# A post-norm decoder layer: x1 and x2 turned by transposing DMA loads instead of by TensorE

## The reference

```python
x1 = layernorm(x  + causal_self_attention(x))        # 16 heads of 32
x2 = layernorm(x1 + cross_attention(x1, ctx))        # one head of 512
# recurrence over the 16 items as time steps, 224 rows as batch:
f = sigmoid(x2[t] @ wf.T + c @ uf.T + bf)
i = sigmoid(x2[t] @ wi.T + c @ ui.T + bi)
g = tanh   (x2[t] @ wc.T + c @ uc.T + bc)
c = f * c + i * g
# output gate, with the last c, for all items:
h = tanh(x2 @ wo.T + c @ uo.T + bo)
out = layernorm(x2 + h)
```

## Time and profile before

| | |
|---|---|
| median of 3 runs | 1476.96 us |
| profiled execution | 1476.7 us, span 1474.8 us, mean granted TensorE clock 0.985 |
| TensorE matmul / weight load | 98% / 85% of the span |
| VectorE / ScalarE / GpSimd | 65% / 43% / 37% |
| DMA | 131.11 MB, 27.8% of 16 engines' span |

### The profile page before, as it was taken

The page is one execution under the profiler, slowest core; times in us unless marked ns, Lnnn a source line. Parts: engine busy times, 40 slices in busy tenths (PEclk is TensorE's granted clock), DMA queues, the critical chain, the costliest instruction groups (busy, mean ns, idle before and its releaser), DMA issues.

```text
span 1474.8 us, 28858 instructions
## 1 busy us (share of the span) xinstructions
PE 1439.7 (98%) x10322; PEld 1254.5 (85%) x10322; DVE 961.9 (65%) x1999; ACT 641.1 (43%) x1890; POOL 541.1 (37%) x429
## 2 busy tenths in 40 slices
PE   6999999999979999999999999999999999999997
PEld 3677777777779999999999999999999999999886
DVE  4578888888767786787778762353455434555697
ACT  4477777777444444444444433322222322222232
POOL 2444555555464656465646552000000000001264
PEclk9899999999999999999999998899999999999999
DMA  6113322324247443334333313200000001000253
GB/s 193 42 52 90 98 76 87 87 80 161 66 155 196 150 156 129 129 129 159 124 130 129 128 32 111 83 26 1 25 25 0 25 0 31 22 7 29 81 192 122
DMA packets 71611, 131.11 MB, mean 89 GB/s; under 512 B 7218, under 2 KB 15410, under 8 KB 71540
## 3 DMA queue, kind: packets, MB, share of 16 engines
q1 hardware_dynamic: 71540, 130.17, 27.8%
HBM read 106.30 MB, written 22.02 MB: 87 GB/s over the span
## 4 chain that ended last, share of the span: by engine, by line
PE 90%; issue 4%; POOL 3%; DVE 2%; SPq 0%; DMA 0%; ACT 0%; POOLq 0%; DVEq 0%
PE banks L1434 15%; PE banks L1453 10%; PE banks L933 9%; PE banks L917 9%; PE banks L307 7%; PE banks L946 6%; PE banks L904 5%; PE banks L1455 5%; PE banks L275 5%; PE banks L256 2%; PE banks L287 2%; PE banks L262 2%; PE banks L235 2%; PE banks L890 2%; POOL o_r L1977 1%
## 5 line engine op out<-in xcount | busy, mean ns | idle before, releaser
L433 ACT ACTIVATE s_p<-banks,a_nmax 112x224 f32<-112x224 f32 (+1 forms) x512 | 198.8, 417 | 94.4 <-DVE a_nmax L519 94.4
L697 POOL TENSOR_TENSOR s_p<-s_p,a_rinv 112x896 f32<-112x896 f32 (+1 forms) x128 | 165.0, 1311 | 166.9 <-DVE a_rinv L527 161.3
L1395 POOL CAST m_hi<-w_raw 128x2048 fp32r<-128x2048 f32 x1 | 2.3, 2257 | 422.6 <-PE banks L1434 422.6
L1638 DVE TENSOR_TENSOR f_gate<-banks,f_xg_early 128x448 f32<-128x448 f32 x45 | 28.1, 624 | 194.4 <-PE banks L1455 194.4
L1257 POOL TENSOR_TENSOR x_cx_lo<-s_cx_raw,x_cx_hi 125x512 fp32r<-125x512 f32 x96 | 120.5, 1292 | 36.1 <-ACT x_cx_hi L1045 36.1
L1543 ACT ACTIVATE f_gate<-f_gate 128x448 f32<-128x448 f32 x90 | 52.1, 579 | 182.5 <-DVE f_gate L1641 182.5
L534 DVE COPY a_pt<-banks 112x448 f32<-112x448 f32 x128 | 79.2, 619 | 61.7 <-PE banks L275 61.6
L433 ACT ACTIVATION_READ_ACCUMULATOR s_p<-banks,a_nmax 112x1 f32 x512 | 113.8, 222 | 0.0
L275 PEld LDWEIGHTS banks<-identity,s_p 112*112 112x112 f32 x768 | 86.6, 134 | 30.5 <-issue 9.3
L275 PE MATMUL banks<-identity,s_p 112*112 112x112 f32 x768 | 106.2, 262 | 0.9 <-DVE a_pt L534 0.9
L518 DVE TENSOR_REDUCE a_nmax<-banks 112x1 f32<-112x224 f32 x256 | 96.8, 378 | 12.6 <-PE banks L262 12.3
(11 more groups left out here) (239 smaller groups left out, 3694.2 us busy)
## 6 DMA issues: line engine op xcount, KB each, us to landing
s_ct_raw<-in_ct SPq DMA_DIRECT2D x16, 1500.0 KB, 6.9
s_cx_raw<-in_cx SPq DMA_DIRECT2D x16, 1500.0 KB
a_xt<-in_xt SPq DMA_DIRECT2D x16, 448.0 KB, 3.9
a_xrow<-in_x SPq DMA_DIRECT2D x16, 448.0 KB, 3.6
a_xres<-in_x SPq DMA_DIRECT2D x16, 448.0 KB, 4.6
x_scratch<-a_xn SPq DMA_DIRECT2D x16, 448.0 KB, 3.1
x_scratch<-x_xn SPq DMA_DIRECT2D x16, 448.0 KB, 3.8
out<-o_y SPq DMA_DIRECT2D x28, 256.0 KB, 2.0
```

The source lines that it names most:

```text
L433: e = act.activation((p1 if c else p0)[:, g, h, :], src, ACT.Exp, bias=nmax[:, g % 2, c, h:h + 1], accum_out=rsum[:, g % 2, c, h:h + 1])
L697: pool.tensor_tensor(p[:, g, :, :], p[:, g, :, :], inv, ALU.mult).then_inc(norm_done, 1)
```

## The change

Beside the fp32 rows, x1 and x2 are now also stored in DRAM as 16-bit halves: `x1_halves` and `x2_halves` have 2T rows for an item, row 2t holding the lower 16 bits of each value of row t and row 2t+1 the upper. A transposing load of such an item, 448 rows by 512 columns of 2-byte elements, leaves on each feature's partition the two halves of each value beside one another, which read as fp32 are the turned item. All `x1_turn` but the first, and `next_turn`, `x_turn` and `turn`, are gone; roundings and low halves read the loaded tile in SBUF, in one instruction of 896 columns instead of two of 448 out of PSUM.

For that: ScalarE separates halves (`separate` for x2, from the normalised item in SBUF, and `separate_ahead` for x1, from an extra load of x1 two items ahead), 2048 columns each, and SyncE stores them. Extra waits keep buffers apart; the load of the wc weight moves from step 2 to the end of cross-attention, since its buffer holds the new tiles. In the softmax the biased maximum and the shift move from VectorE to ScalarE.

In the output gate the turned tiles are loaded 4 slots deep; low halves move from VectorE to GpSimd, the residual from GpSimd to VectorE, and the norm from VectorE to ScalarE, as `y = r * rstd + (-mean * rstd)` with a small instruction for the offset ahead of it; the power of tile n runs one tile earlier in the order. Products use 8 banks instead of 6. The constant -0.5 is made once.

```diff
             def load_rows(b, odd):
                 wait(sp, x1b_done, b - 1)
-                wait(sp, x1t_done, b - 1)
+                if isinstance(b, int) and b in (2, 3):
+                    sp.wait_ge(x1t_done, b - 1)
                 wait(sp, rowbias_done, b - 1)
                 sp.dma_start(x1_raw[odd][:], x1[b].rearrange("(c p) d -> p c d", p=R)).then_inc(x1_in[odd], 16)
 
             def loads(b, odd):
                 wait(sp, ctl_done, KC * b)
                 sp.dma_start(ct_raw[:], io["ct"][b].rearrange("(k p) t -> p k t", p=128)).then_inc(ct_in, 16)
-                if within(b + 1, B):
+                if not (isinstance(b, int) and b == 1):
+                    wait(sp, ahead_stored, 16 * (b - 1))
+                    wait(sp, x1tl_done, b)
+                    if within(b + 1, B):
+                        load_rows(b + 1, 1 - odd)
+                    sp.dma_start_transpose(x1t[:].bitcast(U16), x1_halves[b]).then_inc(x1t_in, 16)
+                elif within(b + 1, B):
                     load_rows(b + 1, 1 - odd)
                 if within(b - 3, B):
                     store(b - 3)
                 wait(sp, cxl_done, XC * b)
                 sp.dma_start(cx_raw[:], io["cx"][b].rearrange("(c p) d -> p c d", p=XR)).then_inc(cx_in, 16)
+                if within(b + 1, B):
+                    wait(sp, ahead_done, b)
+                    sp.dma_start(x1_halves[b + 1].rearrange("(c p w) d -> p c w d", p=R, w=2), ahead_halves[:]).then_inc(ahead_stored, 16)
+                if within(b + 2, B):
+                    rows_ahead(b + 2)
+
+            def rows_ahead(b):
+                sp.dma_start(ahead[:], x1[b].rearrange("(c p) d -> p c d", p=R)).then_inc(ahead_in, 16)
 
             def store(b):
                 sp.wait_ge(xn_done, TC * (b + 1))
                 sp.dma_start(x2[b].rearrange("(c p) d -> p c d", p=R), xn[:]).then_inc(stored, 16)
+                sp.wait_ge(halves_done, b + 1)
+                sp.dma_start(x2_halves[b].rearrange("(c p w) d -> p c w d", p=R, w=2), halves[:]).then_inc(halves_stored, 16)
...
             sp.wait_ge(shared.stored, 16 * B)
+            rows_ahead(2)
...
+            sp.wait_ge(x1tl_done, B)
+            sp.wait_ge(ahead_stored, 16 * (B - 2))
+            load_weight(sp, raw[2], raw_in[2], io["wc_t"])
             for b in range(2):
                 sp.wait_ge(x1b_done, B - 1 + b)
-                sp.wait_ge(x1t_done, B - 1 + b)
                 sp.wait_ge(rowbias_done, B - 1 + b)
-                sp.wait_ge(stored, 16 * (b + 1))
-                sp.dma_start(x1_raw[b][:], x2[b].rearrange("(c p) d -> p c d", p=R)).then_inc(opening.x2_in[b], 16)
...
                     s(b)
-                if within(b + 1, B):
-                    x1_turn(b + 1, 1 - odd, i + 1 + odd)
-                if isinstance(b, int) and b == B:
-                    next_turn(0)
-                    next_turn(1)
+                if isinstance(b, int) and b == 0:
+                    x1_turn(1, 1, 1)
                 if isinstance(b, int) and b == B - 1:
...
+                if not (isinstance(b, int) and b == 1):
+                    wait(act, x1t_in, 16 * (b - 1))
+                    wait(act, zt_done, b)
+                    act.activation(x1t_hi[:], x1t[:], ACT.Copy).then_inc(x1th_done, 1)
+                    return
...
             def exp(b):
                 wait(act, pt_done, XC // 2 * b)
                 wait(act, rinv_done, b)
+                wait(act, rowbias_done, b + 1)
                 for c in range(TC):
+                    wait(act, max_done, TC * b + c + 1)
+                    act.activation(biased_max[:, c:c + 1], smax[:, c:c + 1], ACT.Identity, bias=rowbias[:, c:c + 1]).then_inc(biased_done, 1)
+                    wait(act, biased_done, TC * b + c + 1)
+                    wait(act, exp_done, TC * (b - 1) + c + 1)
+                    act.activation(shift[:, c:c + 1], biased_max[:, c:c + 1], ACT.Identity, scale=-1.0, bias=rowbias[:, c:c + 1])\
+                       .then_inc(shift_done, 1)
                     wait(act, shift_done, TC * b + c + 1)
                     act.activation(p[:, c, :].rearrange("p (a t) -> p a t", a=2), ps_s[0:R, 2 * c:2 * c + 2, 0:XH],
                                    ACT.Exp, bias=shift[:, c:c + 1], accum_out=rsum[:, c:c + 1]).then_inc(exp_done, 1)
 
+            def separate_ahead(b):
+
+                wait(act, ahead_in, 16 * (b - 1))
+                wait(act, ahead_stored, 16 * (b - 2))
+                act.activation(ahead_halves[:], ahead[:].bitcast(U16).rearrange("p c (d w) -> p c w d", w=2), ACT.Copy).then_inc(ahead_done, 1)
+
+            def separate(b):
+
+                wait(act, xn_done, TC * (b + 1))
+                wait(act, halves_stored, 16 * b)
+                act.activation(halves[:], xn[:].bitcast(U16).rearrange("p c (d w) -> p c w d", w=2), ACT.Copy).then_inc(halves_done, 1)
...
                     cxh(b)
+                if within(b - 2, B) and not (isinstance(b, int) and b == B):
+                    separate(b - 2)
+                if within(b, B):
                     exp(b)
                 if within(b + 1, B):
                     x1th(b + 1)
+                if within(b + 2, B):
+                    separate_ahead(b + 2)
...
             def next_columns_low(b):
-                bank = ps_s[:, 2 * b:2 * b + 2, :]
                 dve.wait_ge(opening.xth_done, b + 1)
-                for k in (0, 2):
-                    v = dve.tensor_tensor(opening.xt_lo[:, k:k + 2, b, :], bank[:, k // 2, 0:2 * T].rearrange("p (k t) -> p k t", k=2),
-                                          opening.xt_hi[:, k:k + 2, b, :], ALU.subtract)
-                v.then_inc(opening.xtl_done, 1)
+                dve.tensor_tensor(opening.xt_lo[:, :, b, :], opening.x2t[b][:], opening.xt_hi[:, :, b, :], ALU.subtract)\
...
-                sp.dma_start(x2_raw[:, a, :, :], x2[b].rearrange("(c p) d -> p c d", p=R)).then_inc(x2_in[a], 16)
+                    wait(sp, xtl_done, b - 1)
...
-                act.activation(xt_hi[:, 0:2, a, :], turned(b, 0), ACT.Copy)
-                act.activation(xt_hi[:, 2:4, a, :], turned(b, 2), ACT.Copy).then_inc(xth_done, 1)
+                act.activation(xt_hi[:, :, a, :], x2t[:, a, :, :], ACT.Copy).then_inc(xth_done, 1)
...
+                dve.tensor_tensor(xt_lo[:, :, a, :], x2t[:, a, :, :], xt_hi[:, :, a, :], ALU.subtract).then_inc(xtl_done, 1)
...
-    SLOTS, BANKS = 8, 6
+    SLOTS, BANKS, XT = 8, 8, 4
...
+            def load_turned(n):
+                if n >= TILES:
+                    return
+                if n >= XT:
+                    sp.wait_ge(xtl_done, n - XT + 1)
+                sp.dma_start_transpose(xt[:, n % XT, :, :].bitcast(U16), x2_half_rows[2 * P * n:2 * P * n + 2 * P, :]).then_inc(xt_in[n % XT], 16)
+
+            sp.wait_ge(closing.xtl_done, B)
+            for n in range(XT):
+                load_turned(n)
+            sp.wait_ge(closing.w_split[3], 1)
             for n in range(4):
                 load(n)
-            sp.wait_ge(closing.w_split[3], 1)
+            sp.wait_ge(closing.w_split[4], KC)
             for n in range(4, SLOTS):
                 load(n)
+            for n in range(XT, XT + 3):
+                load_turned(n)
             sp.wait_ge(base_done, 1)
             for j in range(TURNS):
                 for p, q, t, n in pieces(j):
                     sp.dma_start(turned[p:p + n, j, :], base[t:t + n, q, :]).then_inc(turned_in[j // 2], 16)
-            for n in range(SLOTS, TILES):
-                load(n)
+            load_turned(XT + 3)
+            for n in range(SLOTS, TILES + SLOTS):
+                load_turned(n)
+                if n < TILES:
+                    load(n)
                 store(n - SLOTS)
-            for n in range(TILES - SLOTS, TILES):
-                store(n)
             for s in range(4):
                 sp.wait_ge(stored[s], 16 * (TILES // 4))
...
         def xth(act, n):
             if n >= TILES:
                 return
-            act.wait_ge(xt_done, n + 1)
+            act.wait_ge(xt_in[n % XT], 16 * (n // XT + 1))
             if n >= 2:
                 act.wait_ge(o_done, n - 1)
-            act.activation(xt_hi[:, n % 2, :, :], turn_bank(n), ACT.Copy).then_inc(xth_done, 1)
-
-        def xtl(dve, n):
+            act.activation(xt_hi[:, n % 2, :, :], xt[:, n % XT, :, :], ACT.Copy).then_inc(xth_done, 1)
+
+        def xtl(pool, n):
             if n >= TILES:
                 return
-            dve.wait_ge(xth_done, n + 1)
-            dve.tensor_tensor(xt_lo[:, n % 2, :, :], turn_bank(n), xt_hi[:, n % 2, :, :], ALU.subtract).then_inc(xtl_done, 1)
...
+            def norm(n):
+                if n < 0:
+                    return
+                s = n % 4
+                act.wait_ge(rstd_done, n + 1)
+                act.wait_ge(veps_done, 2 * n + 2)
+                act.activation(offset[:, s, :], negative[:, s, :], ACT.Identity, scale=rstd[:, s, :]).then_inc(offset_done, 1)
```

(95 more changed lines are left out.)

213 lines of the change are left out of this document (92 added, 121 removed).

## The result

The changed kernel takes 1470.8 us (median of 5 runs, 1468.2 to 1474.6) against 1476.96: a ratio of 0.9961, 95% interval 0.9943 to 0.9979, so 0.4% faster: 6.2 us by these medians, 5.8 by the ratio. Its profiled execution took 1470.8 us, its span is 1469.1.

The account below looks back on a forecast made before the run. TensorE's own instruction stream was taken to bound cross-attention and recurrence. 1476.7 less 25.5 before the output gate, plus 16.2 in it and 0.3 from profiled execution to median, gave 1467.7, so 1468 us; range 1447 to 1500.

Parts of the forecast that it names:

- Part 1: Cross-attention: TensorE loses the turns of x1 for items 2 to 15, 14 x 0.77 = 10.8 us gained.
- rival C: Cross-attention: the gain is eaten by ScalarE's extra 4.9 us an item, time 1475 to 1479; chance 0.10.
- the turned item is issued behind a 1500 KB load that lands in 6.9 us: Cross-attention: leaves at least 4 us for the 448 KB turning load, 115 GB/s before ScalarE waits.
- Part 2: First cross-attention softmax: TensorE's wait falls from 8.10 to 1.9 us, transposes gain 1.5; together 7.7 gained.
- Part 3: Cross-attention into recurrence: turns of x2 go, but colliding low halves and the late uf load cost more; net 3.4 us lost.
- Part 4: Recurrence: 9.2 us gained from turns of items 4 to 15, about 1.2 from three gate tiles at its end.
- Part 5: Output gate: VectorE's residual and GpSimd's low half collide, a tile every 3.7 us; gate 101.5 us, cost +16.2.
- and directly behind it the next low half 1.24: Output gate: GpSimd's low half directly follows its power, so VectorE's residual waits it out; loop 3.55 us, 3.7 with hand-overs.
- rival A: Output gate: the collision hardly binds; gate 85 us, time 1451 (1445 to 1457); chance 0.17.
- the loop of 7.4 us for two tiles: Output gate, last 12 tiles, lead 1: even without the collision, product through low half and hand-overs take 7.4 us per two tiles.
- B: Output gate: turning loads are slow and transfers bind; time 1503 at 80 GB/s, 1557 at 50; chance 0.22.
- D: Output gate: TensorE, idle a quarter of each tile, gets the lower clock; gate 154 us, time 1520; chance 0.03.

Follow-up runs that it names:

- The split load: Changed kernel with every load of cx_raw issued as two, rows 0 to 111 and 112 to 124 of each chunk, same bytes: 1456.8 us, ratio 0.9872.
- the test alone: Kernel before with only the softmax's biased maximum and shift moved to ScalarE, ahead of the exponential: 1469.57 us, ratio 0.9960.
- The test with uf early: Changed kernel with the load of uf issued ahead of the last two items' stores: 1464.75 us, ratio 0.9921.
- a lead of 2: Changed kernel with LEAD 2 instead of 1 for the output gate's last twelve tiles: 1457.8 us, ratio 0.9882.

## Why the prediction came out near, and which steps failed

1468 against 1470.8 is luck: two terms were wrong by more than 11 us each, with opposite signs. The faster result itself was forecast (9.3 us, about 6 measured), but it is no larger than what the softmax part gains alone.

**Part 1** (10.8 for 14 turns): the term per item is right, 0.82 measured, and ScalarE's extra work was covered, so rival C is out. The step that failed is "the turned item is issued behind a 1500 KB load that lands in 6.9 us". I looked at the load of ct_raw alone. In the same queue stand cx_raw, the store of the halves that the transposing load itself waits for, and at item 3 the weights. In the kernel before, cx_raw delayed nothing that was needed soon; the changed kernel puts a store and a dependent load behind it. The loss at items 2 and 3 was 13 us. The split load shows the cause, since with the same bytes it brings this stretch back to the forecast's length. This failed step is the overlap: the transfers were taken to be hidden behind the item, and for items 2 and 3 they weren't.

**Part 2** (7.7): right, 7.3 in the table and 6.3 by itself. The wait is the 1.9 that was worked out; the 1.5 for the clock came in the changed kernel and not in the test alone. One reading was loose: the addition of 7.09 us was put down to one whole instruction of GpSimd, but it began at 405.36 and outlasted several of them. It waited longer than the rule drawn from it says.

**Part 3**: the net was +3.4 and measured +6.4, with both sizes off. The low halves did collide (6.4 us for two of 896 columns that take 1.1 each elsewhere), but they began at 865.1, earlier than I had them, and the attention product covered most of it: TensorE waited 0.9, not 3.6. The load of uf was at its upper bound: 4.6 of wait, not 1.5, and 2.5 of slow clock behind it that the bound didn't hold. The test with uf early shows it.

**Part 4** (10.4): 12.3 measured, of which 2.1 are the one-column products, 16.21 us instead of 18.30, and no gain of the change. The pair of items takes 59.4 us instead of 61.0.

**Part 5** (+16.2, gate 101.5): +4.9, 90.1. The failed step, as in part 1 one of overlap, is "and directly behind it the next low half 1.24". In the tiles with a longer lead the low half mostly doesn't follow the power: it waits for ScalarE's rounding, and this for the product that frees one of two buffers. VectorE's residual has started by then:
```profile
1421.49 0.69 DVE L1952 TENSOR_TENSOR o_r<-o_h,s_o_x 128x512 f32<-128x512 f32 x1
...
1421.65 1.69 POOL L1874 TENSOR_TENSOR s_o_xt<-s_o_x2t,s_o_xt 128x512 fp32r<-128x512 f32 x1 [0.47 <-ACT s_o_xt L1868]
```
(these two from the kernel with a lead of 2). The engine that starts first keeps its pace, 0.69; the other is held, 1.69 instead of 1.3. Where the changed kernel has them the other way round, GpSimd first, it is VectorE that waits, 1.37 instead of 0.69:
```profile
1388.30 1.30 POOL L1874 TENSOR_TENSOR s_o_xt<-s_o_x2t,s_o_xt 128x512 fp32r<-128x512 f32 x1 [3.09 <-ACT s_o_xt L1868]
...
1388.78 1.37 DVE L1952 TENSOR_TENSOR o_r<-o_h,s_o_x 128x512 f32<-128x512 f32 x1 [1.15 <-ACT o_h L1900]
```
The Trainium skill, "SBUF — State Buffer", Who interferes with whom, says that the order of issue decides who blocks; by this rule the traces agree, and I had used only the half of it in which VectorE loses. So rival A was right for the tiles with a longer lead. In the last twelve the low half does follow the power directly, but the residual hardly meets it: VectorE waits for the product, so from 1427 us on the residual starts within 0.2 us of the low half's end (1427.86, where that ended at 1427.70) and takes 0.68 to 0.72. For these twelve the loop of 7.4 us for two tiles was worked out rightly (3.55 + 3.9 = 7.45), and the test of the lead shows that it costs 11 us.

**Rivals B and D**: transposing loads of 256 KB landed in 4.4 us, four slots deep, and TensorE was full with them running (lead of 2). The Trainium skill, "VectorE: DVE Perf Modes", The three transpose paths, would have made an estimated 10.5 us of each; these loads don't behave as one 128x128 tile after another. The other figure in the prediction, 261 GB/s, is one that the Trainium skill, "DMA: Bandwidth & Descriptors", Latency and other measured facts, gives for a non-contiguous middle dimension, which the prediction left out; the estimate of 1.0 us from it is not what one load took either. For D, the gate's clock was 0.74 from 1379 to 1392 us, where TensorE was busy 9.72 of 13 us, and 1.00 from 1392 to 1461, also where TensorE was busy only 30.88 of 39 us.

**Sum**: the gate 11.3 better than forecast, items 2 and 3 worse by 13.1, the end of cross-attention worse by 3.0, the recurrence better by 1.9, the rest within 1.

## What to carry to other kernels

When work moves from an engine to a transfer, list everything that the queue holds ahead of it, with the time each took to land, not only the load next to it; a slow one that delayed nobody before is now on the path. When two engines share a port, find out which starts first: the order decides who pays, and only the payer's slack matters. A schedule parameter tuned for one distribution of the work (here the lead of 1) has to be tried again after the distribution changes; it hid 11 us of the change's gain. And of a change with several parts each has to be timed alone: here one small part gained as much as all of them together.

## What the runs showed of the hardware

While cx_raw (125 partitions) was landing with little else in flight, from about 416 to 420 us, the DMA engines were 0.3 busy and moved some 129 GB/s; with 112 and 13 partitions the same stretch runs mostly at 0.9 and more. The first answer is the changed kernel from 414 to 433 us, the second the kernel with the split from 413 to 430 (40 slices each, busy tenths and GB/s):
```profile
DMA  9993233333333999789975979999999999997533
GB/s 280 289 254 99 112 134 129 129 129 129 129 129 121 289 280 323 246 259 319 267 160 138 196 192 308 314 256 221 216 210 223 216 219 216 242 215 168 157 125 133
```
```profile
DMA  9999999999999999999997897889999999999999
```
By the Trainium skill, "DMA: Bandwidth & Descriptors", Why a DMA increments its semaphore by 16 and not by 1, that would be 5 of 16 engines, 0.31; the trace agrees. In the steady items the store behind cx_raw lands in 5.1 us (median of 10) with the split and 11.2 (of 11) without.

The issue of a transposing load holds the sync queue: 4.3 to 6.9 us (median 5.8 of 14) for 448 KB in cross-attention, 1.5 to 2.2 for the same size in the recurrence's opening (up to 6.1 later), 1.2 to 2.5 for 256 KB in the gate. What the spread comes from was not measured by itself.
